# The x loads of two passes issued by GpSimd instead of SyncE, in an attention and ternary-weight FFN layer

## The chip, the cores and the metric

The kernel runs on all 8 cores of one Trainium2 chip. Each core works on one of the 8 sequences of the batch and has its own copy of every input; the cores exchange nothing. The metric is the device time of the slowest core, in microseconds. Cores 0 to 3 are one die, cores 4 to 7 the other.

## The reference

```
x = x + attn(layernorm(x), Wq, Wk, Wv, Wo)      # x: 8 x 4096 x 1024, head size 128, causal, one head
x = x + ffn(layernorm(x), w_gate, w_up, w_down) # inner size 4096

def _weight_quant(w):                            # ternary, one scale for a matrix
    scale = 1.0 / jnp.clip(jnp.mean(jnp.abs(w)), 1e-05)
    return jnp.clip(jnp.round(w * scale), -1.0, 1.0) / scale
def _act_quant(x):                               # 8 bit, one scale for a row
    scale = 127.0 / jnp.clip(jnp.max(jnp.abs(x), axis=-1, keepdims=True), 1e-05)
    return jnp.clip(jnp.round(x * scale), -128.0, 127.0) / scale
def _bitlinear(x, w): return jnp.einsum('bsi,oi->bso', _act_quant(x), _weight_quant(w))

ffn = _bitlinear(silu(_bitlinear(x, w_gate)) * _bitlinear(x, w_up), w_down)
```

The mean of |w| over a whole matrix must be known before any of its entries can be quantized, and the mean and the variance of a row of x before it can be normalized.

## The kernel before

A core handles 4096 rows of x as 32 tiles of 128 rows by 1024 columns (fp32, 512 KB each). The whole program is written out by hand: each operation is appended to the list of its engine (`sc.op` with 't' TensorE, 'v' VectorE, 's' ScalarE, 'g' GpSimd, 'q' SyncE, called SP), with the semaphore values that it waits for. An engine runs its list in order, so a DMA whose wait is not met holds up everything behind it in the list of the engine that issues it. All waits are issued by line 966, so the profile gives that line for them.

The stages are, in order:

- *Pass 0* (`for i in range(NT)`, lines 284 to 299). For each tile of x, VectorE sums the rows (L290) and then ScalarE sums the squares in place (L293). x comes in pairs of tiles into two pair buffers, x2_st (the profile's x_st) and a part of qres; `emit_xload_p0pair(k)` loads pair k, and from k = 2 on waits until both tiles of pair k-2 were summed and squared. In the same loop `emit_w1_piece` loads the gate and up weights in 32 pieces of 1 MB and sums their absolute values: even pieces go to the stage wstage and are summed by ScalarE (L233), odd ones to kres and are summed by VectorE (L237). A piece waits until the piece before the last was summed, since that used the same stage.
- The order on SP in this loop is thus: even piece, then x pair, then odd piece, then even piece, then x pair, and so on.
- *Between the passes*, a short chain of small operations turns the sums into mean and 1/deviation for all rows (L301 to L312), two of them on GpSimd (L304, L311).
- *Pass 1* (lines 316 to 335). x is loaded again, tile by tile, into three buffers (`emit_xload_p1p`); ScalarE normalizes a tile (L324), TensorE transposes it (L256), VectorE copies the transposes out of PSUM (L260), TensorE makes Q, K and V (L266, L270, L274), and both engines evict them. The load of tile i+3 waits for the normalization of tile i. The 32 pieces of w_down (512 KB) are loaded and summed in between, again from SP (L228).
- Attention group by group, with a second reading of all weights, which are quantized and kept (gate, up) or written to HBM (down).
- The output projection and the residual, with x read a third time, from GpSimd (L447).
- The FFN: gate and up (L785, L792), then down (L931).

GpSimd has, before pass 0, four DMAs that load the attention weights and cast them to bf16 (L153 to L162). In passes 0 and 1 it has otherwise only L304 and L311; in the attention it multiplies the mask.

```python
    for i in range(NT):
        ...
        if i % 2 == 1 and i // 2 + 2 < NT // 2:
            emit_xload_p0pair(i // 2 + 2)
        if w1_next < 32:
            emit_w1_piece(w1_next)
            w1_next += 1
```

Of the kernel before, what the change touches and what calls it, by code (L numbers as in the profile page):

```python
# [47 lines left out]
def _build():  # L48
# [19 lines left out]
    sc = Sched()  # L68
# [97 lines left out]
    dg_x0 = [None] * NT  # L166
# [5 lines left out]
    def emit_xload_p0pair(k):  # L172
        par = k % 2
        w = []
        if k >= 2:
            w += [('V', v_s1p0[2 * k - 3]), ('S', s_sqa[2 * k - 3])]
        buf = xpair[par]
        sc.op('q', (lambda k=k, buf=buf: (lambda e: e.dma_start(
            out=buf[:, 0:1024], in_=x_d[2 * k * 128:(2 * k + 1) * 128, :])))(),
            waits=w, inc='DQN%d' % par, n=16)  # L180
        v = sc.op('q', (lambda k=k, buf=buf: (lambda e: e.dma_start(
            out=buf[:, 1024:2048], in_=x_d[(2 * k + 1) * 128:(2 * k + 2) * 128, :])))(),
            inc='DQN%d' % par, n=16)
        dg_x0[2 * k] = ('DQN%d' % par, v)
        dg_x0[2 * k + 1] = ('DQN%d' % par, v)

    def emit_xload_p1p(i):
        par = i % 3
        if i >= 3:
            w = [('S', s_lastx[i - 3])]  # L190
        elif i < 2:
            w = [('V', v_s1p0[NT - 4 + i]), ('S', s_sqa[NT - 4 + i])]
        else:
            w = []
        v = sc.op('q', (lambda i=i, par=par: (lambda e: e.dma_start(
            out=x3[par], in_=x_d[i * 128:(i + 1) * 128, :])))(), waits=w, inc='DPX%d' % par, n=16)
        dg_x1p[i] = ('DPX%d' % par, v)

# [85 lines left out]
    v_scale_done = [0]  # L284
    w1_next = 0
    emit_xload_p0pair(0)
    emit_xload_p0pair(1)
    for i in range(NT):
        xs = xpair[(i // 2) % 2][:, (i % 2) * 1024:(i % 2 + 1) * 1024]
        v_s1p0[i] = sc.op('v', (lambda xs=xs, i=i: (lambda e: e.reduce_sum(  # L290
            p0s1[:, i:i + 1], xs, axis=AX)))(), waits=[dg_x0[i]], inc='V')
        sw = [dg_x0[i], ('V', v_s1p0[i])]
        s_sqa[i] = sc.op('s', (lambda xs=xs, i=i: (lambda e: e.activation(  # L293
            xs, xs, AF.Square, accum_out=p0sq[:, i:i + 1])))(), waits=sw, inc='S')
# [5 lines that stand above are left out]
    sc.op('v', lambda e: e.drain())  # L300
    vv = sc.op('v', lambda e: e.tensor_scalar(m_all, p0s1, INV_D, None, ALU.mult),  # L301
               waits=[('S', s_sqa[NT - 1])], inc='V')
# [4 lines left out]
               waits=[('G', gg)], inc='V')  # L307
    ss = sc.op('s', lambda e: e.activation(var_all, var_all, AF.Sqrt, bias=eps_c),
               waits=[('V', vv)], inc='S')
    vv = sc.op('v', lambda e: e.reciprocal(rstd_all, var_all), waits=[('S', ss)], inc='V')  # L310
    gg = sc.op('g', lambda e: e.tensor_mul(bm_all, m_all, rstd_all), waits=[('V', vv)], inc='G')  # L311
    v_chain = sc.op('v', lambda e: e.tensor_scalar(bm_all, bm_all, -1.0, None, ALU.mult),  # L312
                    waits=[('G', gg)], inc='V')
    emit_xload_p1p(0)
    emit_xload_p1p(1)
    emit_xload_p1p(2)
    for i in range(NT):
        par3 = i % 3
# [271 lines left out]
    for g in range(NT // GRP):  # L590
        g0 = g * GRP
        par = g % 2
# [4 lines left out]
        for j in range(GRP):  # L597
# [3 lines left out]
                waits=tw if j == 0 else (), inc='T')  # L601
        t_ot[g] = tt
        v_otev_g[g] = sc.op('v', lambda e: e.tensor_copy(ot_sb, pb[0].bitcast(BF16)[:, 0:512]),  # L603
                            waits=[('T', tt)], inc='V')
# [29 lines left out]
        for j in range(GRP):  # L634
            i = g0 + j
# [3 lines left out]
            if g == 0 and j == 0:  # L639
# [16 lines left out]
            v = sc.op('s', (lambda i=i, xb=xb: (lambda e: e.dma_start(  # L656
                out=x1h_d[i * 128:(i + 1) * 128, :], in_=xb)))(),
                waits=[('V', vv)], inc='DSX%d' % pari, n=16)
            ds_x1[i] = ('DSX%d' % pari, v)
            if j >= 1:  # L660
# [4 lines left out]
               waits=[('V', v_stats[NT - 1])], inc='S')  # L665
# [80 lines left out]
    for i in range(NT):  # L746
        par = i % 2
# [11 lines left out]
        for c in range(HC):  # L759
# [3 lines left out]
                waits=tw if c == 0 else (), inc='T')  # L763
# [7 lines left out]
        for qtr in range(4):  # L771
# [10 lines left out]
            for c in range(HC):  # L782
                for half in range(2):
# [6 lines left out]
                        waits=tw if first else (), inc='T')  # L790
# [9 lines left out]
            if qtr >= 1:  # L800
# [5 lines left out]
                waits=[('S', s_silu_q[(i, qtr)])], inc='V')  # L806
# [11 lines left out]
            if qtr == 1 and i >= 1:  # L818
# [5 lines left out]
                for c in range(OC):  # L824
# [5 lines left out]
                        waits=tw2 if c == 0 else (), inc='T')  # L830
                sw2 = [('T', tt2)]
                if i >= 2:
# [3 lines left out]
                    waits=sw2, inc='S')  # L836
                ss2 = sc.op('s', (lambda fu=fu: (lambda e: e.activation(
                    nqt_sb[:, 2048:4096], fu.bitcast(BF16)[:, 0:2048], AF.Identity)))(),
                    inc='S')
# [6 lines left out]
            if qtr == 1 and i + 1 < NT:  # L846
# [14 lines left out]
                   waits=[('V', v_stt_q[(i, 3)])], inc='V')  # L861
        s_nqh_t[i] = sc.op('s', lambda e: e.activation(nqh_sb, h_sb, AF.Identity, bias=ng_c),  # L862
                           waits=[('V', vv)], inc='S')
# [3 lines left out]
    for c in range(OC):  # L867
# [5 lines left out]
            waits=tw2 if c == 0 else (), inc='T')  # L873
    sw2 = [('T', tt2), ds_nq[NT - 2]]
    ss2 = sc.op('s', lambda e: e.activation(nqt_sb[:, 0:2048], pb[0].bitcast(BF16)[:, 0:2048], AF.Identity),
                waits=sw2, inc='S')
    ss2 = sc.op('s', lambda e: e.activation(nqt_sb[:, 2048:4096], pb[1].bitcast(BF16)[:, 0:2048], AF.Identity),
                inc='S')
    v2 = sc.op('s', lambda e: e.dma_start(out=nqh_d[NT - 1], in_=nqt_sb),
               waits=[('S', ss2)], inc='DSN', n=16)  # L880
# [11 lines left out]
    v = sc.op('q', lambda e: e.dma_start(  # L892
        out=wdq_sb.rearrange("p (c d) -> p c d", c=OC),
        in_=wdqh_d.rearrange("c p d -> p c d")),
        waits=[('T', t_E[NT - 1]), ds_wd_done], inc='DQWD', n=16)
# [25 lines left out]
    for i in range(NT):  # L921
        par = i % 2
# [6 lines left out]
        for c in range(OC):  # L929
            for half in range(2):  # L930
# [5 lines left out]
                    waits=tw if (c == 0 and half == 0) else (), inc='T')  # L936
        t_down[i] = tt
        vw = [('T', tt), dq_x1pb[i]]
        if i >= 2:
# [8 lines left out]
        v = sc.op('s', (lambda i=i, par=par: (lambda e: e.dma_start(  # L948
            out=y_d[i * 128:(i + 1) * 128, :], in_=out_sb[par])))(),
            waits=[('V', vv)], inc='DSY%d' % par, n=16)  # L950
# [53 lines left out]
```

How the kernel before makes its waits and increments, by code:

```python
        def body(eng):  # L961
            last = {}
            for fn, waits, inc, n in sc.st[key]:
                for s, v in waits:
                    if last.get(s, 0) < v:
                        eng.wait_ge(sems[s], v)
                        last[s] = v
                inst = fn(eng)
                if inc is not None:
                    inst.then_inc(sems[inc], n)
```

## Time and profile before

| what | value |
|---|---|
| median of 3 runs | 2812.66 us (2811.61 to 2813.88) |
| the profiled execution | 2813.85 us |
| its span on the slowest core, core 1 | 2812.1 us |
| spans of the other cores | 2793.7 to 2808.8 us |
| busy share of the span | PE 61%, DVE 33%, ACT 29%, POOL 1% |
| DMA queue of SP (q1) | 210.85 MB, 22.8% of 16 engines |
| DMA queue of ACT (q10) | 76.55 MB, 6.8% |
| DMA queue of GpSimd (q0) | 17.83 MB, 2.5% |

PE is TensorE, DVE VectorE, ACT ScalarE, POOL GpSimd, SP SyncE. A busy share is an average over stages with very different limits, so each stage is read by itself. All times in rows are microseconds from the span's start. The name behind a line number is the tile that is written, then an arrow, then what is read.

### The profile page before, as it was taken

Reading aid. Unit: us, or ns where it says so; the run is one execution under the profiler, and the core shown is the slowest. Engines: PE = TensorE matmul, PEld = TensorE weight load, DVE = VectorE, ACT = ScalarE, POOL = GpSimd, SP = SyncE. Lnnn points to the kernel's source line nnn. Section 1 sums busy time; section 2 is a strip of 40 time slices with the busy share of each in tenths; the row PEclk is TensorE's granted clock in tenths of the full one; section 3 lists DMA queues with packets and bytes.
Section 4 is the critical chain, followed back from the end, with each engine's and each line's share of the span. In section 5 each row is a group of like instructions: output and inputs, shape, how many; then the busy total and the mean of one; then the engine's idle time right before and its main releaser. Section 6 shows DMA issues by size and latency. Waiting matters only on the chain.

```text
span 2812.1 us, 25064 instructions; the slowest of 8 cores (2793.7 to 2812.1 us)
## 1 busy us (share of the span) xinstructions
PE 1702.9 (61%) x9618; PEld 880.3 (31%) x9618; DVE 936.8 (33%) x1358; ACT 804.6 (29%) x734; POOL 33.6 (1%) x74
## 2 busy tenths in 40 slices
PE   0001555123221247778778777877877785999999
PEld 0000444122220023333334333333433332444444
DVE  1323222551224744343443434344343431111111
ACT  1223222664432223333333333333333331000000
POOL 0000000000000100000000000000000000000000
PEclk9999555556665579999999999999999997999999
DMA  6455443863336830011001001100100006444443
GB/s 182 192 214 199 152 156 130 264 226 104 94 103 203 259 109 30 38 46 45 30 38 45 30 38 45 45 31 38 45 31 38 38 31 209 150 150 151 156 157 121
DMA packets 74598, 306.83 MB, mean 109 GB/s; under 512 B 10864, under 2 KB 12912, under 8 KB 58096
## 3 DMA queue, kind: packets, MB, share of 16 engines
q1 hardware_dynamic: 47024, 210.85, 22.8%
q10 hardware_dynamic: 19584, 76.55, 6.8%
q0 software_dynamic: 7872, 17.83, 2.5%
q8 instruction: 77, 1.26, 0.2%
q14 instruction: 41, 0.34, 0.0%
HBM read 229.70 MB, written 76.55 MB: 109 GB/s over the span
## 4 chain that ended last, share of the span: by engine, by line
PE 56%; DMA 13%; DVE 11%; issue 9%; ACT 8%; DVEq 2%; SPq 1%; POOL 0%; ACTq 0%; POOLq 0%
PE pb L785 17%; PE pb L792 17%; PE pb L931 16%; DMA wdqh<-wdq_st 4%; DVE h_sb L804 3%; ACT kres L802 3%; DMA kres<-wgt 2%; DMA kres<-wut 2%; DVE st_cols L809 1%; ACT nqh_sb L324 1%; ACT wdq_st L412 1%; PE pb L496 1%; PE pb L471 1%; PE pb L266 1%; PE pb L256 1%
## 5 line engine op out<-in xcount | busy, mean ns | idle before, releaser
L785 PE MATMUL pb<-wgq,qres 128*128 128x512 bf16 x2048 | 806.9, 394 | 287.9 <-DVE qres L768 253.3
L792 PE MATMUL pb<-wuq,qres 128*128 128x512 bf16 x2048 | 805.0, 393 | 0.0
L931 PE MATMUL pb<-wdq_sb,nqt_in 128*128 128x512 bf16 x2048 | 444.6, 380 | 22.2 <-DMA nqt_in<-nqh 22.2
L804 DVE SCALAR_TENSOR_TENSOR h_sb<-pb,st_cols,kres 128x1024 f32<-128x1024 f32 x128 | 164.3, 1284 | 735.0 <-ACT kres L802 735.0
L785 PEld LDWEIGHTS pb<-wgq,qres 128*128 128x128 bf16 x2048 | 206.8, 101 | 552.0 <-issue 333.0
L792 PEld LDWEIGHTS pb<-wuq,qres 128*128 128x128 bf16 x2048 | 205.5, 100 | 252.5 <-issue 32.7
L802 ACT ACTIVATE kres<-pb,st_cols 128x1024 f32<-128x1024 f32 x128 | 142.9, 1116 | 494.0 <-PE pb L792 332.0
L931 PEld LDWEIGHTS pb<-wdq_sb,nqt_in 128*128 128x128 bf16 x2048 | 200.9, 98 | 265.6 <-issue 25.6
L256 PE MATMUL pb<-ident_sb,nqh_sb 128*128 128x128 bf16 x256 | 30.7, 294 | 337.4 <-ACT nqh_sb L324 337.4
L496 PE MATMUL pb<-qres,kres 128*128 128x128 bf16 x528 | 52.5, 260 | 240.0 <-ACT pt L514 225.6
L862 ACT ACTIVATE nqh_sb<-h_sb,konst 128x4096 bf16<-128x4096 f32 x32 | 118.8, 3711 | 215.9 <-DVE h_sb L860 215.9
L941 DVE SCALAR_TENSOR_TENSOR out_sb<-pb,c_all,x_in 128x512 f32<-128x512 f32 x32 | 24.0, 751 | 430.9 <-PE pb L931 430.9
L809 DVE TENSOR_REDUCE st_cols<-h_sb 128x1 f32<-128x1024 f32 x128 | 156.2, 1220 | 12.1 <-issue 0.4
L256 PEld LDWEIGHTS pb<-ident_sb,nqh_sb 128*128 128x128 bf16 x256 | 23.4, 132 | 344.7 <-issue 344.7
L496 PEld LDWEIGHTS pb<-qres,kres 128*128 128x128 bf16 x528 | 42.2, 119 | 245.7 <-issue 242.8
L237 DVE TENSOR_REDUCE wsums<-kres 128x1 f32<-128x2048 f32 x16 | 36.6, 2286 | 175.4 <-DMA kres<-wgt 100.7
L860 DVE TENSOR_SCALAR h_sb<-h_sb,st_cols,konst 128x4096 f32<-128x4096 f32 x32 | 77.2, 2412 | 5.6 <-DVE c_all L858 5.6
L734 ACT ACTIVATE qres<-ln_scr,konst 128x1024 bf16<-128x1024 f32 x32 | 36.8, 1151 | 130.8 <-DVE ln_scr L727 130.8
L641 PE MATMUL pb<-wo_sb,ot_sb 128*128 128x512 bf16 x32 | 19.0, 593 | 90.4 <-DVE ot_sb L603 88.5
L834 ACT ACTIVATE nqt_sb<-pb 128x2048 bf16<-128x2048 bf16 x31 | 58.2, 1878 | 21.0 <-PE pb L827 21.0
L514 ACT ACTIVATE pt<-pb,konst 128x1024 bf16<-128x1024 f32 x56 | 59.1, 1119 | 10.4 <-PE pb L496 5.1
L827 PE MATMUL pb<-ident_sb,nqh_sb 128*128 128x128 bf16 x992 | 60.4, 219 | 0.0
(152 smaller groups left out, 1368.4 us busy)
## 6 DMA issues: line engine op xcount, KB each, us to landing
nqh<-nqt_sb ACTq DMA_DIRECT2D x32, 1024.0 KB, 3.9
nqt_in<-nqh SPq DMA_DIRECT2D x32, 1024.0 KB, 5.3
x_st<-x SPq DMA_DIRECT2D x38, 512.0 KB, 3.8
x_st<-x1h SPq DMA_DIRECT2D x32, 512.0 KB, 3.3
x_in<-x1h SPq DMA_DIRECT2D x32, 512.0 KB, 6.9
y<-out_sb ACTq DMA_DIRECT2D x32, 512.0 KB, 7.0
wstage<-wgt SPq DMA_DIRECT2D x12, 1024.0 KB, 9.2
wstage<-wut SPq DMA_DIRECT2D x12, 1024.0 KB, 8.8
```

The costliest lines, as they stand in the source:

```text
L256: tt = sc.op('t', (lambda c=c, par=par, src_ln1=src_ln1: (lambda e: e.transpose(psA[par][:, c * 128:(c + 1) * 128], src_ln1[:, c * 128:(c ...
L496: tt = sc.op('t', (lambda k=k, q=q, pbst=pbst, off=off, j=j: (lambda e: e.matmul(pbst[:, off + j * 128: off + (j + 1) * 128], kres[:, k * ...
L514: s_exp_last[pp] = sc.op('s', (lambda pp=pp, ptx=ptx: (lambda e: e.activation(pt_row[ptx][:, 0:1024], pb[pp][:, 0:1024], AF.Exp, scale=sms ...
L785: tt = sc.op('t', (lambda c=c, o0=o0, gb=gb, half=half, par=par: (lambda e: e.matmul(gb[:, half * 512:(half + 1) * 512], xqTb[par][:, c * ...
L792: tt = sc.op('t', (lambda c=c, o0=o0, ub=ub, half=half, par=par: (lambda e: e.matmul(ub[:, half * 512:(half + 1) * 512], xqTb[par][:, c * ...
L802: s_silu_q[(i, qtr)] = sc.op('s', (lambda gb=gb, i=i: (lambda e: e.activation(g_s, gb, AF.Silu, scale=c1g_p[i % 2])))(), waits=sw, inc='S')
L804: v_stt_q[(i, qtr)] = sc.op('v', (lambda qtr=qtr, ub=ub, i=i: (lambda e: e.scalar_tensor_tensor(h_sb[:, qtr * 1024:(qtr + 1) * 1024], ub, ...
L809: sc.op('v', (lambda qtr=qtr: (lambda e: e.reduce_max(mh4[:, qtr:qtr + 1], h_sb[:, qtr * 1024:(qtr + 1) * 1024], axis=AX, apply_absolute_v ...
L827: tt2 = sc.op('t', (lambda c=c, pbx=pbx, coff=coff: (lambda e: e.transpose(pbx.bitcast(BF16)[:, coff:coff + 128], nqh_sb[:, c * 128:(c + 1 ...
L860: vv = sc.op('v', lambda e: e.tensor_scalar(h_sb, h_sb, s2q_c, cb_c, ALU.mult, ALU.add), waits=[('V', v_stt_q[(i, 3)])], inc='V')
L862: s_nqh_t[i] = sc.op('s', lambda e: e.activation(nqh_sb, h_sb, AF.Identity, bias=ng_c), waits=[('V', vv)], inc='S')
L931: tt = sc.op('t', (lambda c=c, half=half, par=par: (lambda e: e.matmul(dps[par][:, half * 512:(half + 1) * 512], nqt_in[par][:, c * 128:(c ...
```

## The change

Three DMA issues move from SP's list to GpSimd's: the two of a pair in pass 0 and the one of a tile in pass 1. What they wait for is unchanged. The pass 0 loads now count on the semaphores DGX0 and DGX1, which the third reading of x, later in the program, also uses.

```diff
@@ emit_xload_p0pair
-        sc.op('q', (lambda k=k, buf=buf: (lambda e: e.dma_start(
+        sc.op('g', (lambda k=k, buf=buf: (lambda e: e.dma_start(
             out=buf[:, 0:1024], in_=x_d[2 * k * 128:(2 * k + 1) * 128, :])))(),
-            waits=w, inc='DQN%d' % par, n=16)
-        v = sc.op('q', (lambda k=k, buf=buf: (lambda e: e.dma_start(
+            waits=w, inc='DGX%d' % par, n=16)
+        v = sc.op('g', (lambda k=k, buf=buf: (lambda e: e.dma_start(
             out=buf[:, 1024:2048], in_=x_d[(2 * k + 1) * 128:(2 * k + 2) * 128, :])))(),
-            inc='DQN%d' % par, n=16)
-        dg_x0[2 * k] = ('DQN%d' % par, v)
-        dg_x0[2 * k + 1] = ('DQN%d' % par, v)
+            inc='DGX%d' % par, n=16)
+        dg_x0[2 * k] = ('DGX%d' % par, v)
+        dg_x0[2 * k + 1] = ('DGX%d' % par, v)
@@ emit_xload_p1p
-        v = sc.op('q', (lambda i=i, par=par: (lambda e: e.dma_start(
+        v = sc.op('g', (lambda i=i, par=par: (lambda e: e.dma_start(
             out=x3[par], in_=x_d[i * 128:(i + 1) * 128, :])))(), waits=w, inc='DPX%d' % par, n=16)
```

## Rows read from the trace of the kernel before

**Rows 1.** Stretches, core 1: PE, PEld, DVE, ACT, POOL busy; clock, DMA share, GB/s.

```profile
26.60:251.00 224.40, 0.00 (x0) 0.00 (x0) 63.79 (x43) 57.19 (x84) 0.00 (x0) 1.00 0.54 201
```

**Rows 2.** Waits of SP's queue, core 1: total us, times, longest.

```profile
SPq L966 <- DVE p0s L290: 150.7, 14, 12.9
```

**Rows 3.** Timeline, core 1, one round of pass 0: start, duration, engine, line.

```profile
117.44 2.29 DVE L237 TENSOR_REDUCE wsums<-kres 128x1 f32<-128x2048 f32 x1 [11.26 <-DMA kres<-wgt]
119.64 2.33 DVE L290 TENSOR_REDUCE p0s<-x_st 128x1 f32<-128x1024 f32 x2
120.94 1.06 ACT L293 ACTIVATE x_st<-x_st 128x1024 f32<-128x1024 f32 x1 [11.71 <-DVE p0s L290]
...
122.00 1.89 ACT L233 ACTIVATE wstage<-wstage 128x2048 f32<-128x2048 f32 x1
...
125.10 0.33 SPq L178 DMA_DIRECT2D x_st<-x  x1
...
125.94 0.43 SPq L228 DMA_DIRECT2D kres<-wgt  x1
...
133.26 2.29 DVE L237 TENSOR_REDUCE wsums<-kres 128x1 f32<-128x2048 f32 x1 [11.28 <-DMA kres<-wgt]
```

**Rows 4.** Stretches of 2 us, core 0, columns as in rows 1.

```profile
122.00:124.00 2.00, 0.00 (x0) 0.00 (x0) 0.00 (x0) 0.00 (x0) 0.00 (x0) 1.00 1.06 440
```

**Rows 5.** The same stretch on core 1.

```profile
122.00:124.00 2.00, 0.00 (x0) 0.00 (x0) 0.00 (x0) 2.00 (x4) 0.00 (x0) 1.00 0.00 0
```

**Rows 6.** One early stretch on every core: cores 0, 1, 4 and 5.

```profile
28.00:36.00 8.00, 0.00 (x0) 0.00 (x0) 2.55 (x2) 0.00 (x0) 0.00 (x0) 1.00 0.94 306
...
28.00:36.00 8.00, 0.00 (x0) 0.00 (x0) 0.00 (x0) 0.00 (x0) 0.00 (x0) 1.00 0.98 273
...
28.00:36.00 8.00, 0.00 (x0) 0.00 (x0) 0.86 (x1) 0.00 (x0) 0.00 (x0) 1.00 1.02 268
...
28.00:36.00 8.00, 0.00 (x0) 0.00 (x0) 0.00 (x0) 0.00 (x0) 0.00 (x0) 1.00 0.97 266
```

**Rows 7.** The chain that ended last, end of pass 0: start, us, what.

```profile
243.01 2.30 DVE wsums L237
...
245.38 5.26 DMA kres<-wut
...
250.74 2.30 DVE wsums L237
...
259.68 2.29 DVE wsums L237
```

**Rows 8.** DMA queues and landings, 0 to 26 us, and two timeline rows.

```profile
q0 software_dynamic: 3264, 1.05, 40.0%
...
wo_sb<-wo POOLq DMA_DIRECT2D x1, 256.0 KB, 21.8
...
4.34 0.58 POOL L162 DMA_DIRECT2D wo_sb<-wo  x1
...
13.88 2.35 DVE L290 TENSOR_REDUCE p0s<-x_st 128x1 f32<-128x1024 f32 x2 [11.35 <-DMA x_st<-x]
```

**Rows 9.** Timeline, core 1, between the passes.

```profile
264.10 0.25 POOL L311 TENSOR_TENSOR bm_all<-m_all,rstd_all 128x32 f32<-128x32 f32 x1 [1.31 <-DVE rstd_all L310]
...
264.73 1.24 ACT L324 ACTIVATE nqh_sb<-x_st,bm_all,rstd_all 128x1024 bf16<-128x1024 f32 x1 [1.23 <-DVE bm_all L312]
```

**Rows 10.** GpSimd's x loads of the later stage, line 447; ScalarE's waits, line 233.

```profile
L447 POOL DMA_DIRECT2D x_st<-x x16: 528/528/612, 874.6 to 987.0; - x16
...
DMA to landing us min/median/max: 4.1/5.9/7.9
...
  DMA nqh_sb<-wdt: 2.1, 3
```

**Rows 11.** Timeline, core 1, one tile of pass 1.

```profile
424.56 1.23 ACT L324 ACTIVATE nqh_sb<-ln_scr,bm_all,rstd_all 128x1024 bf16<-128x1024 f32 x1
...
427.05 0.69 DVE L260 COPY nqt_sb<-pb 128x1024 bf16<-128x1024 bf16 x1 [3.27 <-PE pb L256]
```

## Prediction

> **What bounds the kernel now.** I read the busy time by stretches first [rows 1]. Pass 0, the first 262 us, reads 48 MB (x once, the gate and up weights once) and does nothing else. In its body all 16 DMA engines are busy only 0.54 of the time and move 201 GB/s, vector and scalar engine are busy about a quarter of it each, and TensorE is idle. So nothing in that stretch is full. It is bound by a cycle of waits, and the change lies in that cycle.
>
> The waits of the DMA queue on SyncE (SP) name it [rows 2]: SP stands 150.7 us, 14 times, before issuing because vector has not yet reduced an x tile (the line is the loop that emits waits). The timeline shows one round of the cycle, two x tiles and two weight pieces [rows 3]. SP issues at 125.10 the next x pair and only behind it, at 125.94 and right after, the two 1 MB weight pieces. The odd piece (stage kres) lands for vector at 133.26. Vector sums it (2.29), then two tiles (2.33); scalar follows: square 1.06 from 120.94, sum of the even piece 1.89 from 122.00, then the second tile's square. Only then can SP pass its x wait. From 117.44 to 133.26 is 15.8 us, of which 7.7 us pass from the sum's start to the next issue and 8.2 us in flight. The stage kres was free at 119.7, but its reload stood in the queue behind an x load that waited for scalar until 125.1. That is head-of-line blocking of about 6 us in 15.8.
>
> The stretches of 2 us show how this sits beside the other core of a pair [rows 4, 5]: at 122 to 124 core 0 moves 440 GB/s while core 1 moves nothing. Each core works while the other loads. Where both load, in the 8 us from 28 on, no core gets that [rows 6]: 306+273 = 579 GB/s for cores 0 and 1, 268+266 = 534 for cores 4 and 5. So about 270 GB/s a core is what remains when both want to stream. This is the figure that will size the gain.
>
> **The change, part by part.** All 32 tiles of pass 0 and all 32 of pass 1 are loaded by GpSimd's queue instead of SP's. Bytes, buffers and conditions of release are the same; the waits are the same but the queue behind them is another. What is behind SP's wait now: the weight pieces. What is behind GpSimd's: the next x load, and two small multiplies between the passes.
>
> *Steady rounds.* Without the x wait SP needs for the odd piece only vector's sum and its own earlier even piece, which needs scalar's sum. So one piece is in flight while the other is summed, and the x pair (issued by GpSimd after the second square, as now) fills the rest. Is a chain of waits left that is longer than the bytes? The last two rounds of pass 0 have no x load ahead, and there a piece is issued, lands after 5.26 and is summed in 2.3, a round of 7.7 us; the next is 8.9 [rows 7]. So the chains could run at about 8 us. The bytes cannot: a round is 3 MB = 3.146e6 bytes, at 270 GB/s 11.7 us. Laying out a round by hand (even piece and x pair share the engines for 7.8 us, the odd piece has them for 3.9) the next even piece is issued 0.8 us before the odd one is through and the next x pair about when it is, so 0.6 us or so has nothing in flight. I take 12.3. Bounds: at the 579 of cores 0 and 1 10.9+0.6 = 11.5; and if both pieces fall into step, so that a core loads nothing for 4 us a round and its partner has 420 in that time, 3.146 = 4×0.42+(T-8)×0.27, T = 13.4.
>
> The HBM Reference of the Trainium skill (Specifications) states about 358 GB/s a core when both cores of a pair stream; no row here shows it, the nearest are the 266 to 306 of [rows 6]. By it a round would be 8.8+0.6 = 9.4 us; this is a rival below, priced from the chains.
>
> *Start.* GpSimd has four weight loads with a cast ahead of its first x load, 1 MB in 3264 small packets, 40.0% of the 16 engines' time in the first 26 us, i.e. 10.4 us, the last landing 21.8 us after its issue at 4.34 [rows 8]. The x tiles now queue behind them. They get the engines in turn with two weight pieces (2.1e6 bytes, 7.8 us at 270). From 2.6, when the first packets can run (estimated from the last of the four issues at 4.34): 2.6+10.4+7.8 = 20.8, then half a MB (1.9) and some 1.8 to land: the first reduce at 24.5 instead of 13.88 [rows 8]. Then 1.2 to scalar, table load and first square 2.5, the piece 2.1: the second even piece is issued at 30.4, the odd at 30.8, x pair 2 at 31.6. Its odd piece lands after 11.7 and some 2 at 44.5, its sum ends at 46.8. Late bound: the casts end only when they do now, 26.1, +5 us.
>
> *Sum of pass 0.* 46.8, then 12 rounds of 12.3 = 147.6, then two rounds without x at 8.3 (mean of the two now [rows 7]) = 16.6: 211. It ends now at 259.68+2.29 = 261.97. Gain 51 us.
>
> *Between the passes.* SP issues the first three tiles of pass 1 long before the statistics are ready. On GpSimd they stand behind its second multiply (264.10, 0.25) [rows 9]. From its end the first LayerNorm activation now follows 0.4 us later; then it follows an issue (0.53) and a landing, 4.1 to 7.9, median 5.9, for the same shape from this queue [rows 10]. I take 0.5+4.4-0.4 = 4.5 us lost, once; bounds 4.2 and 8.
>
> *Pass 1.* A tile is issued three tiles ahead of its use, some 20 us, and lands in 6: hidden. SP's weight pieces of pass 1 are issued earlier; scalar waited for them 2.1 us in all [rows 10], so at most that is gained, and I count nothing. The one cost that could lie on the chain: GpSimd generates the descriptors itself. The SBUF page (SBUF — State Buffer, Who interferes with whom) says that vector's two-port copies and GpSimd lock each other out for a whole instruction. In the rows, GpSimd would start at the end of the LayerNorm activation (424.56+1.23) and be done 0.53 later, at 426.4, while the copy of the transposes starts at 427.05 [rows 11]. They miss each other by 0.6 us, so nothing is counted; if they always met it would be 32×0.53 = 17 us. Pass 0's vector work is reductions only, and beside such reductions the issue takes 528 at median and 528 at least [rows 10].
>
> Everything after pass 1 keeps its instructions. Net: 51-4.5 = 46.5. The profiled execution took 2813.85 us (span 2812.1); 2767.3, and less the 1.2 us by which it is above the median of the runs, **2766 us**.
>
> **Rivals.**
> - *The pair carries more* than 540 GB/s. The 440 of one core alone [rows 4] and the 579 speak for some of it, [rows 6] against much. If rounds come down to near 9.3 us, 12×3.0 = 36 and 4 at the start and end: 2726. Chance 0.08.
> - *Little is freed:* SP still stands at the even piece, which needs scalar, and both fall back into step. The Trainium skill's DMA page (DMA: Bandwidth & Descriptors, Issuing engines are not separate DMA queues) says that a second issuing engine saves only issue time. From the rows that is 125.94-125.10 = 0.84 us in 14 rounds, 12 us, less 4.5 and up to 5 at the start: 2805 to 2810. Against it: what is taken away is a wait in order, about 6 us a round. Chance 0.07. Half-way cases (rounds of 13.4 to 15) 0.08: 2780 to 2800.
> - *Slower:* the software queue starves beside SP's two pieces. In the first 26 us its 1 MB took until 26.1, some 23.6 us. If an x pair took near that, rounds are bound by it: 13×11.3 = 147 more, 2913. It decides from 12.3+46.5/13 = 15.9 us a pair. Against it: those packets are small (320 bytes on average), and whole tiles from this queue land in 5.9 at median with the engines three quarters busy. Chance 0.07.
>
> **Numbers.** The forecast has 0.70. A measurement here can tell about 0.2%, 5.6 us. Its own range: rounds of 11.5 give 2756, of 13.4 2780, the late start 2785, some meeting of copy and issue 2795. With part of the first rival below, the range is 2742 to 2796, which leaves out about 2 in 10. Faster 0.89, within 0.2% 0.04 (part of the second rival), slower 0.07.
>
> **What would show it.** Right: the last sum of pass 0 ends near 211 us; kres pieces are issued within 0.5 us of vector's sum or of the even piece; between two kres sums 11.5 to 13.4 us; in the body of pass 0 the DMA share is above 0.9 and the rate near 260 GB/s, on both cores of a pair at once; first x reduce near 24; first LayerNorm activation 5 us behind GpSimd's second multiply; pass 1's tiles still 6.9 us apart; later stages unchanged in length. Wrong: a DMA share that stays at 0.55, tiles of x that land later than 15 us after issue, or copies L260 longer than 0.69 us.

## The result and the profile after

The changed kernel takes 2739.95 us (median of 8 runs, 2736.35 to 2743.91) beside 2812.45 of before (8 runs): ratio 0.9744, interval 0.9732 to 0.9756, 72.5 us faster. The forecast was 2766 with a range of 2742 to 2796. The direction and the mechanism were right; the gain is half as large again as forecast, and the time lies 2 us below the range. The profiled execution took 2743.08 us; its slowest core is now core 5. In some executions one die runs at a lower clock and takes longer; where that makes the median of an experiment unsteady, the stages of its profiled execution are compared instead.

The stretch of 100 us in the body of pass 0, cores 1 and 5 of the changed kernel (columns as in [rows 1]):

```profile
60.00:160.00 100.00, 0.00 (x0) 0.00 (x0) 45.38 (x30) 41.33 (x61) 10.48 (x20) 1.00 0.97 315
...
60.00:160.00 100.00, 0.00 (x0) 0.00 (x0) 44.99 (x30) 40.33 (x59) 9.43 (x18) 1.00 0.96 309
```

The DMA share that was 0.54 [rows 1] is 0.97, the rate 315 instead of 201 GB/s. The DMA engines, idle almost half of the time before, are now nearly full. All eight cores show 0.94 to 0.97 and 304 to 316 GB/s from 60 to 180 us, so both cores of a pair stream at once, where [rows 4, 5] showed one standing while the other loaded.

The waits of SP in pass 0 (0 to 194 us), changed kernel, core 5:

```profile
SPq L966 <- ACT wstage L233: 95.4, 15, 33.3
SPq L966 <- DVE wsums L237: 76.0, 14, 6.7
```

The waits for an x tile are gone. They were more than the 150.7 us of [rows 2], which are those that ended with VectorE's sum: 48.7 us more on core 1 of the kernel before (27.6 and 21.1) ended with ScalarE's square, 199 us in all. SP now waits for the sum of the stage that it wants to refill. The timeline of one round, core 4 of the changed kernel, beside [rows 3]:

```profile
98.56 2.29 DVE L237 TENSOR_REDUCE wsums<-kres 128x1 f32<-128x2048 f32 x1 [5.07 <-DMA kres<-wgt]
100.77 2.33 DVE L290 TENSOR_REDUCE p0s<-qres 128x1 f32<-128x1024 f32 x2
100.92 0.33 SPq L228 DMA_DIRECT2D kres<-wgt  x1
...
103.12 1.89 ACT L233 ACTIVATE wstage<-wstage 128x2048 f32<-128x2048 f32 x1
104.92 0.19 ACT L233 ACTIVATION_READ_ACCUMULATOR wstage<-wstage 128x1 f32 x1
...
105.18 0.33 SPq L228 DMA_DIRECT2D wstage<-wut  x1
...
106.70 0.53 POOL L178 DMA_DIRECT2D qres<-x  x1 [8.56 <-ACT qres L293]
...
109.10 2.29 DVE L237 TENSOR_REDUCE wsums<-kres 128x1 f32<-128x2048 f32 x1 [6.00 <-DMA kres<-wgt]
```

The odd piece is issued 0.07 us after its stage is free (98.56+2.29 = 100.85), the even one 0.07 after ScalarE read its sum out (104.92+0.19 = 105.11), the x pair by GpSimd 1.5 us later. One round is 10.5 us here. The chain that ended last, core 5, has the same shape to the end of pass 0, with the first x tile and the seam to pass 1:

```profile
5.41 25.00 DMA x_st<-x
...
30.51 1.23 DVE p0s L290
...
48.33 2.30 DVE wsums L237
...
172.01 2.30 DVE wsums L237
...
183.42 2.30 DVE wsums L237
...
191.86 2.29 DVE wsums L237
...
196.28 0.24 POOL bm_all L311
...
196.79 4.11 DMA x_st<-x
...
201.04 1.25 ACT nqh_sb L324
```

Pass 0 ends at 191.86+2.29 = 194.15 us, 68 us earlier than at [rows 7]. Over the eight cores the last odd sum starts at 184.7 us on average, before at 256.8: 72.1 us. From there to the first normalization 9.3 instead of 5.1 us pass (+4.2), pass 1 from its first to its last normalization is 212.3 instead of 214.5 us (-2.2), and from there to the last issue of the down matmuls 2317.6 instead of 2320.4 (-2.8). So the gain is pass 0's; the other three nearly cancel (-0.8).

### The profile page after: what moved, and what is told of

Its sections match the earlier page's. It is cut to its first block, busy times and chain, and to the rows that moved or that the text cites. A ratio compares the mean times of both kernels' runs of the same rounds, so it can differ in the third digit from the quotient of the medians.

```text
span 2741.3 us, 25106 instructions; the slowest of 8 cores (2718.7 to 2741.3 us)
## 1 busy us (share of the span) xinstructions
PE 1705.1 (62%) x9618; PEld 879.2 (32%) x9618; DVE 936.5 (34%) x1358; ACT 803.0 (29%) x734; POOL 67.3 (2%) x138
## 4 chain that ended last, share of the span: by engine, by line
PE 58%; DMA 13%; DVE 12%; ACT 8%; issue 6%; DVEq 2%; POOL 1%; ACTq 0%; SPq 0%; POOLq 0%
PE pb L785 18%; PE pb L792 17%; PE pb L931 16%; DMA wdqh<-wdq_st 5%; DVE h_sb L804 3%; ACT kres L802 3%; DMA kres<-wgt 2%; DMA kres<-wut 2%; DMA x_st<-x 2%; DVE st_cols L809 1%; ACT nqh_sb L324 1%; ACT wdq_st L412 1%; DVE wsums L237 1%; PE pb L256 1%; PE pb L266 1%
```

## The experiments

For each I give the steady round: the time from the 4th to the 14th sum of an odd piece, divided by 10, mean of the eight cores. It is 15.63 us in the kernel before and 10.04 in the changed one. Times come from three sets of runs, each with its own runs of before, 2807.5 to 2808.6 us there: e1 to e4, then c1 and e5 to e7, then e8 and e9. The stages come from one profiled execution of each kernel.

**The two moves apart.**

```diff
 e1: from the changed kernel            e2: from the kernel before
 def emit_xload_p1p                     def emit_xload_p1p
-    sc.op('g', ...)                   -    sc.op('q', ...)
+    sc.op('q', ...)                   +    sc.op('g', ...)
```

> Only pass 0's x loads on GpSimd; pass 1's stay on SP. If the whole gain of the change (72.5 us, to 2740) comes from the order in pass 0, it stays, and the 4.1 us that pass 1's first tile loses behind GpSimd's second multiply come back, less about 2 us that SP's weight pieces of pass 1 then wait again: 2738, between 2735 and 2741. If pass 1's move carries part of the gain, 2745 or more.

> Only pass 1's x loads on GpSimd; pass 0 as before. By the same theory 4.1 us lost at the first tile and 2 gained: 2815 beside 2812.5 of before (slower by 2, within what can be told). If the move in pass 1 were a gain of its own: 2808 or less.

e1: 2747.69 us, ratio 0.9789 (0.9738 to 0.9839), but three of its six times are 2733 to 2735 and three 2760 to 2772, so the time can't tell 2738 from 2745: three lie at the lower end of the expected band or just below it, three above 2745. The stages can: steady round 9.72, last odd sum at 179.1, first normalization 5.1 us behind it (9.3 in the changed kernel), pass 1 216.0 us (212.3). So the move in pass 1 costs 4.2 us at the seam and gives 3.7 back in pass 1. e2 agrees: 2808.29, ratio 1.0006 (0.9979 to 1.0034), steady round 15.6 as before, 4.3 us lost at the seam and 2.8 won in pass 1 (211.7). What pass 1's move is worth is too small to show in the time; the expectation had the sizes within 2 us.

e1 also says how far a stage can be trusted. Its pass 0 is the changed kernel's, yet its last odd sum is 5.6 us earlier than there (184.7; 183.0 in c1 below). Differences of a few us between the ends of pass 0 of two profiled executions therefore show nothing.

**The order on one queue.** e3 leaves every load on SP and swaps two statements of the loop:

```diff
     for i in range(NT):
+        if w1_next < 32:
+            emit_w1_piece(w1_next)
+            w1_next += 1
         if i % 2 == 1 and i // 2 + 2 < NT // 2:
             emit_xload_p0pair(i // 2 + 2)
-        if w1_next < 32:
-            emit_w1_piece(w1_next)
-            w1_next += 1
```

> All loads stay on SP; in pass 0 the weight piece is issued ahead of the x pair, so the odd piece no longer waits for ScalarE's last square. Theory A (it is the order on one queue, not the queue): pass 0's rounds fall from 15.8 us to 10.3 to 11 as with GpSimd, and the first reduce stays at 14 us instead of 30.5: 2725 to 2740. Theory B (two queues move more than one): rounds stay above 12 us and the time is above 2765.

2774.7 us, ratio 0.9837 (0.9791 to 0.9884); its times scatter from 2751.6 to 2803.6, so the median lies in B's band and the lowest times between the two. The steady round is 11.71 us (11.61 to 11.76 on the cores): also between the bands of A and B. Neither theory was whole. Of the 5.6 us a round that the change saves, the order alone gives 3.9; the other 1.7 need the second queue. The timeline of e3, core 1, says why:

```profile
103.95 1.91 ACT L233 ACTIVATE wstage<-wstage 128x2048 f32<-128x2048 f32 x1 [4.58 <-DMA wstage<-wgt]
...
105.86 1.04 ACT L293 ACTIVATE qres<-qres 128x1024 f32<-128x1024 f32 x1
106.42 2.29 DVE L237 TENSOR_REDUCE wsums<-kres 128x1 f32<-128x2048 f32 x1 [7.17 <-DMA kres<-wgt]
...
107.07 0.33 SPq L178 DMA_DIRECT2D qres<-x  x1
...
107.91 0.43 SPq L228 DMA_DIRECT2D wstage<-wut  x1
...
108.78 0.33 SPq L228 DMA_DIRECT2D kres<-wut  x1
```

ScalarE had summed the even piece at 105.9, but its reload stands behind the x pair until 107.91, and all three loads are again issued within 2 us. The two pieces land within some 2.5 us (ScalarE starts on its piece at 103.95, VectorE on its own at 106.42), and until the next loads get going nothing is in flight. The pair partly takes turns again: from 100 to 105 us core 1 moves 434 GB/s and core 0 118. A stretch of 1 us there, and the body of e3, both core 1:

```profile
106.00:107.00 1.00, 0.00 (x0) 0.00 (x0) 0.58 (x1) 0.99 (x2) 0.00 (x0) 1.00 0.00 0
...
60.00:160.00 100.00, 0.00 (x0) 0.00 (x0) 40.84 (x27) 35.62 (x52) 0.00 (x0) 1.00 0.72 267
```

**The kind of queue.** e5 issues pass 0's x from ScalarE, behind the second square, and pass 1's from SP. c1 is the changed kernel again, in the same set of runs.

```diff
 def emit_xload_p0pair
-    sc.op('g', ... inc='DGX%d' % par, n=16)   # both DMAs of the pair
+    sc.op('s', ... inc='DSY%d' % par, n=16)
 def emit_xload_p1p
-    sc.op('g', ...)
+    sc.op('q', ...)
```

> The changed kernel itself, as the yardstick for the kernels beside it on this chip: 0.974 of before, and in pass 0 rounds of 10.3 us, a DMA share of 0.95 and 304 to 316 GB/s on every core.

> Pass 0's x loads issued by ScalarE, right behind the second square, pass 1's on SP. Theory A (what counts is that x and the weight pieces stand in different queues, of which kind does not matter): rounds of 10 to 10.5 us and a DMA share above 0.9; the x tiles are no longer behind the casts, but by the byte count that is worth only the idle engine time at the start, so 2728 to 2734. Theory B (GpSimd's queue as such moves more): rounds above 11 us, 2745 or more.

c1: 2736.23, ratio 0.9733 (0.9703 to 0.9763), steady round 9.88, 315 to 323 GB/s. e5: 2728.69, ratio 0.9721 (0.9678 to 0.9763), steady round 9.93; its body, core 1:

```profile
60.00:160.00 100.00, 0.00 (x0) 0.00 (x0) 46.25 (x31) 42.88 (x63) 0.00 (x0) 1.00 0.96 320
```

Same round, share and rate as with GpSimd, and the time is in A's band: theory A. That it is another queue counts, not which of these two. e5's median is 7.5 us below c1's, but the intervals overlap. Its stages would fit such a lead: the last odd sum at 174.2 instead of 183.0 (179.1 in e1), and no 4 us at the seam.

**The start.** e4 places the four cast loads behind the first two x pairs:

```diff
-    sc.op('g', ... out=wq_sb ...)   # and wk_sb, wv_sb, wo_sb
 ...
     emit_xload_p0pair(0)
     emit_xload_p0pair(1)
+    sc.op('g', ... out=wq_sb ...)   # and wk_sb, wv_sb, wo_sb
```

> The changed kernel with the four cast loads behind the first two x pairs on GpSimd. Theory A (pass 0 is bound by the DMA engines' time, the casts must be moved anyway): only the idle stretch of the engines at the start comes back, 6 to 9 us: 2731 to 2734. Theory B (a delay of the first reduce is a delay of the end): the first reduce at about 13 instead of 30.5 us, all of it gained: 2723.

2734.59, ratio 0.9756 (0.9715 to 0.9797). The first x reduce starts at 14.8 us instead of 28.2, mean of the cores, but the last odd sum at 180.9 instead of 184.7: 13.4 us earlier at the start leave 3.8 at the end, which is within what e1 and the changed kernel differ by. Theory B is out. A was right that most of the lead is lost; whether anything of its 6 to 9 us is there, these runs don't tell. The timeline, core 1, shows where the lead goes:

```profile
16.30 2.28 DVE L226 TENSOR_REDUCE wsums<-kres 128x1 f32<-128x2048 f32 x1
...
20.17 1.81 SPq L217 DMA_DIRECT2D kres<-wgt  x1
...
39.79 2.29 DVE L226 TENSOR_REDUCE wsums<-kres 128x1 f32<-128x2048 f32 x1 [18.51 <-DMA kres<-wgt]
```

The second odd piece now travels beside the casts' small packets, an even piece and an x pair, and needs 19.6 us. A longer first round (23.2 us between the first two odd sums instead of 13.7, mean of the cores) takes the place of the late start.

**Bytes or chain?** Three kernels aim at one of the two at a time.

```diff
 e6, from the third pair on (both tiles):
-    out=buf[:, 0:1024], in_=x_d[rows, :]
+    out=buf[:, 0:512],  in_=x_d[rows, 0:512]     # squares go to ln_scr
 e7, ahead of each odd piece's sum in pass 0:
+    sc.op('v', lambda e: e.reduce_sum(st[:, 30:31], dstap, ...))
 e9, behind each x pair from the third on, twice:
+    sc.op('g', lambda e: e.dma_start(out=xt[:, xo:xo + 512], in_=x_d[rows, 0:512]))
```

> The changed kernel with half of each x tile loaded from the third pair on (columns 512 to 1023 keep old contents, so the statistics are not those of x), the squares written to another buffer. A round moves 2.62e6 bytes instead of 3.15e6; vector and scalar do the same work. Theory A (pass 0 is bound by bytes at about 312 GB/s a core): rounds of 8.4 to 8.8 us, 13 rounds, 20 to 24 us less than the changed kernel. Theory B (the chain piece landing, sum, reload is what is left): rounds stay at 10.2.

> The changed kernel with VectorE summing each odd piece of pass 0 twice (2.3 us more in each of 16 rounds, result unused). Theory A (bound by bytes): rounds stay within 0.6 us of 10.3, at most 9 us in all. Theory B (bound by the chain of the odd stage): 2.3 us a round, 35 us in all.

> The changed kernel with two more loads of 256 KB per x pair from the third pair on, into SBUF that nothing uses then (data unused): 3.67e6 instead of 3.15e6 bytes a round. Theory A (at this size the rounds are bound by bytes): the whole price at 318 GB/s a core, 1.65 us a round, rounds of 11.8 to 12.0 us, 23 us in all over 14 pairs. Theory B (rounds are bound by the chain and bytes have room, as the smaller effect of half the x bytes could mean): under 0.8 us a round.

The bodies of e6, e7 and e9, core 1, in this order:

```profile
60.00:160.00 100.00, 0.00 (x0) 0.00 (x0) 50.06 (x34) 45.52 (x66) 10.65 (x20) 1.00 0.83 288
```

```profile
60.00:160.00 100.00, 0.00 (x0) 0.00 (x0) 61.85 (x38) 36.71 (x54) 9.43 (x18) 1.00 0.88 285
```

```profile
60.00:160.00 100.00, 0.00 (x0) 0.00 (x0) 40.84 (x27) 37.64 (x57) 19.13 (x36) 1.00 0.99 333
```

| kernel | bytes a round | steady round | against c1 (9.88) | time | ratio |
|---|---|---|---|---|---|
| e6, half x | 2.62e6 | 9.13 | -0.75 | 2740.96 | 0.9749 (0.9707 to 0.9791) |
| e7, sum twice | 3.15e6 | 11.01 | +1.13 | 2753.5 | 0.9786 (0.9746 to 0.9827) |
| e9, more bytes | 3.67e6 | 11.28 | +1.40 | 2755.22 | 0.9804 (0.9776 to 0.9833) |

Neither of the two pure theories holds. With half the x bytes the engines are no longer full (0.83 to 0.89) and the round stops at 9.1, above the 8.4 to 8.8 of theory A: something other than bytes binds there, and the chain of landing, summing and reloading is what is left. The sum of 2.3 us more costs half of its price, so the chain has about 1.2 us of room at 9.9. With more bytes the engines are full all the time and nearly the whole price is paid, 1.40 of 1.65 us. (e9's x sums also wait for the added loads, which count on the same semaphore, so its chain is longer too; with the engines never idle it is the bytes that bind.) e9 gives the size that the prediction lacked: on six cores 330 to 335 GB/s at a share of 0.99 to 1.00, so two cores of a pair that never stop move about 665 GB/s. Their rounds are 11.0 to 11.3 us, what 3.67e6 bytes take at 332 GB/s (11.1). The fourth pair, cores 6 and 7, got 309 and 317 at the same share (rounds 12.06 and 11.57), and why is open. At 332 GB/s the changed kernel's bytes need 3.146/0.332 = 9.5 us of its 10.0. Bytes and chain lie within 1 us of each other. (e6's time is no less than c1's, though 20 to 24 us less were expected; its last odd sum is 12.9 us earlier, 170.1 against 183.0. The slowest core of its profiled execution, core 0, lost the lead behind pass 1: 2349.8 us from its last normalization to the end, 2319.9 to 2333.9 on the others. Why is open; on the stages alone rests what e6 says here. e9 ran in another set than c1; e8, in e9's set, has 9.82.)

**A better version.** e8 takes e1 and e4 together.

```diff
 def emit_xload_p1p
-    sc.op('g', ...)
+    sc.op('q', ...)
 # and the four cast loads behind emit_xload_p0pair(1), as in e4
```

> Pass 0's x on GpSimd with the casts behind its first two pairs, pass 1's x back on SP. From the changed kernel this should gain what each part gave: about 4 us from pass 1's first tile, 0 to 4 us from the casts, so 2728 to 2734, ratio 0.969 to 0.973. If a part is lost to the other: 0.974 or above.

2734.1, ratio 0.973 (0.9708 to 0.9752), at the edge of what was expected if both parts gain. The steady round is 9.82 and the first normalization comes at 181.7 instead of 192.1 us (c1), yet on the time it isn't told apart from the changed kernel, whose ratio is 0.9733 to 0.9744. The same goes for e5. Whether one of the two is really some us faster stays open.

## Why the prediction fell short

*What binds.* Right: pass 0 was bound by the x load at the head of SP's queue, and e3 shows the order alone to be worth 3.9 of 15.6 us a round.

*Steady rounds.* Here the prediction failed, in the term "a round is 3 MB = 3.146e6 bytes, at 270 GB/s 11.7 us". The gap of 0.6 us beside it was good: the rounds are 10.0 to 10.3, of which bytes take 9.5. The rate was wrong: 304 to 316 GB/s are kept up, and 332 when never idle, not 270. I took it from one stretch of 8 us in the first rounds [rows 6]. The DMA share could not have warned of it: it is 0.94 to 1.02 there at 266 to 306 GB/s, and 0.99 to 1.00 in e9 at 330 to 335. The prediction set against it the page of the Trainium skill that it names (HBM Reference, Specifications: about 358 GB/s a core). e9 lies 7% below the Trainium skill's figure and 23% above mine; the measurement decides, and the skill's was the nearer one. Twelve rounds at 10.31 instead of 12.3 (48.33 to 172.01, core 5) are 24 us, of which the start and the end of pass 0 below take 7 back. The rival that the pair carries more got 0.08, with 9.3 us a round: it was closer to the truth than the forecast. What made the early stretch slower was not tried. The first rounds of the changed kernel, 13.7 and 12.5 us on average, are also longer than the rest, and the second of them begins long after the casts: on core 5 the last cast landed at 27.9 us and that round begins at 48.33. So it is not the casts' tail alone.

*Start.* The first reduce was forecast at 24.5 and came at 30.51 on core 5 (28.2 on average). The casts and the x tiles behind them took longer than the sum had it; the second odd piece's sum ended at 50.6, not 46.8, +3.8. e4 shows that a late first reduce costs little: the casts' time is paid in the first round then.

*End of pass 0.* The last two rounds took 19.85 us (172.01 to 191.86), not 16.6, +3.3. The three terms add up: 211-24+3.8+3.3 = 194.1. Core 5 is the latest of the eight; on their mean pass 0 gained 72.1 us instead of 51, which is 21 of the 26 us by which the forecast missed. The rest, on the same mean, is 0.3 at the seam, 2.2 in pass 1 and 2.8 behind it.

*Between the passes.* Forecast 4.5 us lost, measured: from the end of GpSimd's multiply (196.28+0.24) to the normalization 4.5 us, 0.4 before, 4.1 lost; the load landed in 4.1.

*Pass 1.* Nothing was counted; -2.2 us came. ScalarE's waits for w_down pieces, of which [rows 10] shows core 1's 2.1 us and which come to 0.7 to 8.8 us on the eight cores, are gone on all of them in the changed kernel; in e1, with pass 1's x on SP, they are back (0.8 to 10.9). The prediction had read one core. The lock between GpSimd and VectorE's copies that the prediction takes from the Trainium skill (SBUF — State Buffer, Who interferes with whom) did not show; the copies, changed kernel, core 5:

```profile
L260 DVE COPY nqt_sb<-pb x32: 690/691/693, 203.7 to 417.1; 128x1024 bf16<-128x1024 bf16 x32
```

That is 0.69 us each as in [rows 11], and GpSimd's issues took 528 ns at median. The prediction let GpSimd issue right at the end of the normalization and so had a distance of 0.6 us; the issue starts 0.55 us later than that, and most tiles miss by 0.18 us only. In 10 tiles of the eight cores the two overlap by 0.22 us, as here on core 3:

```profile
204.33 0.53 POOL L195 DMA_DIRECT2D x_st<-x  x1 [7.05 <-ACT nqh_sb L324]
204.64 0.69 DVE L260 COPY nqt_sb<-pb 128x1024 bf16<-128x1024 bf16 x1 [2.80 <-PE pb L256]
```

Neither is longer than elsewhere, so where they met nothing was lost. Whether this copy, which reads PSUM, is one of the two-port copies that the Trainium skill speaks of is on no row.

*Rivals.* "Little is freed" by the rule of the Trainium skill that a second issuing engine saves only issue time (DMA: Bandwidth & Descriptors, Issuing engines are not separate DMA queues): refuted, 5.6 us a round against the 0.84 of issue. As a rule on bandwidth it agrees, since GpSimd's and ScalarE's queue give the same rate. But in e3, on one queue and in the better order, 1.7 us a round are still lost to waits in order. "Slower" did not come: in pass 0, core 5, the first tile of a pair landed in 7.4 us at median and the second in 9.3. Only the tiles issued beside the casts took as long as that rival feared, up to 26.5 us; from 40 us on no tile on any core took more than 13.0.

## What to carry to other kernels

If a stage's engines and its DMA are both half idle, look at what stands at the head of the issuing queue: a load whose wait ends late blocks loads whose buffers are free, and loads that are then issued together land together and are consumed with nothing in flight. Streams with their own release conditions want their own queue; reordering on one queue gave most of it here, 3.9 of 5.6 us a round, not all. The gain is then bounded by bytes at the rate that two cores reach together, and this rate wants a long stretch in which both stream, not one of the first rounds.

## What the runs showed of the hardware

A core alone moved 440 GB/s in 2 us [rows 4], while its pair partner stood. With both streaming all the time it was 330 to 335 GB/s a core on three pairs and 309 and 317 on the fourth (e9); in the first rounds 266 to 306 [rows 6]. All of these are at a DMA share of 0.94 or more, so the share does not tell the rate. A 1 MB piece beside the four casting loads, another piece and an x pair took 19.6 us to land (e4); in the changed kernel, core 5, such a piece took 6.6 to 9.1 once the casts were through. The casts' 1 MB comes in 3264 packets of some 320 bytes and holds the DMA engines 10 us [rows 8]. A GpSimd issue and a VectorE copy from PSUM that overlapped by 0.22 us kept their 0.53 and 0.69 us (changed kernel, 10 tiles).
